# First edge stage of a two-layer graph network on one Trainium2 core: index columns and relative node columns held in SBUF and copied per chunk

## The chip, the cores and the metric

The kernel runs on one core of one Trainium2 chip. The metric is the device time of one execution in microseconds (us). The engines of the core are TensorE (PE), VectorE (DVE), ScalarE (ACT) and GpSimd (POOL); SyncE (SP) issues transfers. Transfers issued by SP and ACT and those issued by POOL run on the same 16 DMA engines.

## What is computed

The reference is two graph transformer layers over 6250 nodes of 256 features, with 206,250 edges sorted by destination. The part that this change touches is the first layer's edge attention:

```
src, dst = edges in order of dst                # 206250
s = einsum('edh,edh->eh', q[rows], k[cols])     # rows = dst, cols = src, 8 heads of 32
m = segment_max(s, rows);  e = exp(s - m[rows])
z = segment_sum(e, rows);  attn = e / z[rows]
out = segment_sum(attn[:, None, :] * v[cols], rows)
x = x + out @ Wo + bo + mix(xn)
```

After it come a routed feed-forward layer, a second layer with a mean over neighbours, linear attention and a second routed layer whose gates come from a graph attention over 139,264 edges. None of that is touched.

## The kernel before

The program is a row of stages. The ones that matter here lie between 860 and 4260 us of the span:

- `plan_steps` (L646 to L820) cuts the sorted edges into steps of 256 edges, each inside one window of 128 destination nodes, and makes the tables that the edge stage reads. On PE it transposes two of them (L741), so that a table with one step per partition becomes one with an edge of a tile per partition: the destination relative to the window (`rel`, written to `turned` negated, L817) and the source node (`lsf`, written to `turned_i` as integers, L819). Both are 128 partitions by 1792 columns of four bytes, one column per tile of 128 edges. SP writes them to DRAM as `SRCI` and `RELT` (L713, L714) and the stage ends when five such writes have landed (L715).
- `window_masks` (from L823) is a small stage that makes constants.
- `edge_attention` (L857 on) is the first edge stage. It runs over 107 chunks of 16 tiles of 128 edges (8 steps). `chunks` (L900) writes two chunks in front, a loop with two chunks in its body, and the last few at the end. All buffers of a chunk are double (index `s`).

What each engine does for a chunk, in the order of its own program:

- SP (`ahead`, `behind`, L929 to L942) reads with DMA: `oht`, the relative nodes of 2048 edges broadcast to all partitions (1 MB); `idx`, 16 columns of `SRCI` (L934); `relt`, 16 columns of `RELT` (L936); then `t3` and `flg` for the scans (L940, L941). Each waits until the chunk two before has released its buffer.
- POOL (`gather`, L960) fetches key and value rows of the source nodes: 16 indirect DMAs (L965), each with 128 rows of 2080 bytes, whose row numbers are one column of `idx`. It first waits for `idx` to land (L961). Each four gathers wait until PE has used up the four tiles two chunks earlier (`agg_ps`, L963). So a chunk has two stretches of eight gathers: groups 0 and 1, which are free once PE has done the first sums of the same-parity chunk before it, and groups 2 and 3, freed in the following body.
- ACT makes one-hot matrices with Abs and Relu: of `oht` (L977, L982) and of the nodes per tile (`far_edges`, L991, with a column of `relt` as bias; `mask_edges`, L998). It also takes the exponential (L1036, L1037) and copies the sums out of PSUM (`keep`, L1002).
- PE expands the queries of the window (L1067), transposes scores (L1074) and weights (L1113), spreads carries (L1101, L1106), makes the factor of a continued window (L1118, L1119), and sums messages (L1082, L1083, L1087); `agg_ps` counts the last of these.
- DVE multiplies and reduces scores (L1145, L1147), scans for the maxima (L1153 to L1177), weighs values (L1192) and rescales the open window (L1182, L1199).

The order on each engine is written out by hand. On ACT, in the body of chunk i, the first two of the 16 L991 of chunk i+1 stand between a `keep` and the exponential of chunk i; the wait for `relt` stands ahead of them. `at(eng, sem, c, per, i)` (L639) waits until chunk c has reached its count; inside the loop it is a wait against a register. `loaded` (L58) is the same for a DMA.

Of the kernel before, what the change touches and what calls it, by code (L numbers as in the profile page):

```python
# [57 lines left out]
def loaded(eng, sem, t, s, per=1, slots=2):  # L58


    wait_reg(eng, sem, (t - s) * (16 * per // slots) + 16 * per)
# [584 lines left out]
def plan_steps(nc, k, w):  # L646

    with ExitStack() as c:
# [17 lines left out]
        flg = sb("flg", [P, SC, 2, 4])  # L666
        turned = sb("turned", [P, NSP, 2])
        turned_i = sb("turned_i", [P, NSP, 2], I32)
        psA = c.enter_context(nc.psum_tensor("p_psA", [P, 512], F32))
# [17 lines left out]
        def _(sp):  # L687
# [24 lines left out]
            sp.wait_ge(turn_sb, 2)  # L712
            sp.dma_start(k.SRCI, turned_i[:].rearrange("p s g -> p (s g)")).then_inc(kept, 16)  # L713
            sp.dma_start(k.RELT, turned[:].rearrange("p s g -> p (s g)")).then_inc(kept, 16)  # L714
            sp.wait_ge(kept, 16 * 5)  # L715

# [140 lines left out]
def edge_attention(nc, k, w):  # L857
# [5 lines left out]
    with ExitStack() as c:  # L863
# [22 lines left out]
        set_done, table_in, q_in, zeroed = sem("set_done"), sem("table_in"), sem("q_in"), sem("zeroed")  # L886
        rel_in, t3_in, flg_in, idx_in, relt_in = ([sem(f"{n}_in{s}") for s in range(2)] for n in (
            "rel", "t3", "flg", "idx", "relt"))
        kv_in = [[sem(f"kv_in{s}_{g}") for g in range(4)] for s in range(2)]
# [5 lines left out]
            "exp_done", "oht_done", "oh_done", "oht_abs", "oh_abs", "fac_done"))  # L895
        x_step = sem("x_step")
        block = c.enter_context(nc.Block())
# [27 lines left out]
        @block.sync  # L925
        def _(sp):
            sp.dma_start(acc[:, 1:NT + 1, 0:C], k.Q.rearrange("(t p) c -> p t c", p=P)).then_inc(q_in, 16)

            def ahead(i, s):  # L929
                at(sp, q_ps, i - 2, 4, 3)  # L930
                sp.dma_start(oht[:, s, :], k.REL.rearrange("s e -> (s e)")[bass.ds(i * CT * P, CT * P)].partition_broadcast(P))\
                    .then_inc(rel_in[s], 16)
                at(sp, s_done, i - 2, 4, 3)
                sp.dma_start(idx[:, s, :], k.SRCI[:, bass.ds(i * CT, CT)]).then_inc(idx_in[s], 16)  # L934
                at(sp, oh_done, i - 2, 2, 1)
                sp.dma_start(relt[:, s, :], k.RELT[:, bass.ds(i * CT, CT)]).then_inc(relt_in[s], 16)  # L936

            def behind(i, s):
                at(sp, x3_done, i - 2, 1, 0)
                sp.dma_start(t3[:, s, :], k.T3D[bass.ds(i * CT, CT), :].unsqueeze(1).to_broadcast([CT, HEADS, TW])).then_inc(t3_in[s], 16)  # L940
                sp.dma_start(flg[:, s].rearrange("p t f -> p (t f)"),  # L941
                             k.FLG.rearrange("t f -> (t f)")[bass.ds(i * CT * 4, (CT + 1) * 4)].partition_broadcast(HEADS)).then_inc(flg_in[s], 16)  # L942
            ahead(0, 0)
            ahead(1, 1)
            behind(0, 0)

            def body(i, s):
                if inside(i + 2):
                    ahead(i + 2, s)
                if inside(i + 1):  # L950
                    behind(i + 1, 1 - s)
            chunks(sp, body)

        @block.gpsimd
        def _(pool):
            pool.memset(acc[:, NT + 1, :], 0.0).then_inc(zeroed, 1)
            pool.memset(acc[:, 0, :], 0.0).then_inc(zeroed, 1)
            pool.memset(acc[:, 1:NT + 1, C:VW], 0.0).then_inc(zeroed, 1)

            def gather(i, s):  # L960
                loaded(pool, idx_in[s], i, s)  # L961
                for g in range(4):
                    at(pool, agg_ps, i - 2, CS, 2 * g + 1)  # L963
                    for t in range(4 * g, 4 * g + 4):
                        pool.indirect_dma_start(kv[:, s, t, :], None, k.KV,  # L965
                                                bass.IndirectOffsetOnAxis(ap=idx[:, s, t:t + 1], axis=0)).then_inc(kv_in[s][g], 16)
            chunks(pool, gather)

        @block.scalar
        def _(act):  # L970
# [13 lines left out]
            def far_edges(i, s, tiles):  # L984
                if tiles[0] == 0:
                    loaded(act, relt_in[s], i, s)
                    at(act, agg_ps, i - 2, CS, CS // 2 - 1)
# [1737 lines left out]
def program(nc, w, out, scratch):  # L2725
    k = Core()
    with ExitStack() as c:
# [12 lines left out]
        k.REL, k.T3D = scratch("REL", [NSP, STEP]), scratch("T3D", [2 * NSP, TW])  # L2740
        k.FLG, k.SRCI, k.RELT = scratch("FLG", [2 * NSP, 4]), scratch("SRCI", [P, 2 * NSP], I32), scratch("RELT", [P, 2 * NSP])
        k.STEPB, k.STEPI, k.FIRST = scratch("STEPB", [NSP]), scratch("STEPI", [NSP], I32), scratch("FIRST", [NSP])
# [23 lines left out]
        with ExitStack() as cg:  # L2766
# [3 lines left out]
            with ExitStack() as ce:  # L2770
                k.QA = ce.enter_context(nc.sbuf_tensor("QA", [P, NT + 2, VW], F32))
                with ExitStack() as cw:
                    k.step_i, k.step_r = (cw.enter_context(nc.sbuf_tensor(n, [1, NSP], I32)) for n in ("step_i", "step_r"))
                    k.selh, k.maskj, k.selT, k.negpart = (cw.enter_context(nc.sbuf_tensor(n, s, F32)) for n, s in (
# [45 lines left out]
```

## Time and profile before

| | us |
|---|---|
| Median of 3 runs (13223.25 to 13242.68) | 13238.97 |
| The profiled execution, whole | 13243.9 |
| Its span, first to last instruction | 13242.3 |
| First edge stage, first SP issue to last L991 start | 951 to 4235 |
| Busy in the whole span: PE / DVE / ACT / POOL | 6677 / 6328 / 2226 / 6040 |

The page's busy shares are means over stages with different limits: none of the engines is over half busy in the whole span. The chain that ended last, in the page, is that of the final feed-forward stage and says nothing of the edge stage. What bounds the edge stage has to be read from the waits and the order of events in it. In rows of the trace, a bracket such as `[4.69 <-PE e_psA L1087]` gives the idle time ahead of the instruction and what ended it; `issue` stands for time in which nothing visible was waited for, `remote` for a semaphore that came long after the instruction that raises it seemed done.

### The profile page before, as it was taken

The page shows a single profiled execution, that of the slowest core. Times are in us where ns is not written, and L with a number is a line of the kernel's source. Part 1 is how long each engine was busy: PE and PEld are TensorE (multiplying, and loading weights), DVE is VectorE, ACT ScalarE, POOL GpSimd, SP SyncE. Part 2 cuts the span into 40 slices and gives each one's busy share as a digit, 9 for nine tenths or more (in the row PEclk, how much of TensorE's full clock was granted, in tenths as well). Part 3 has the DMA queues.
Part 4 walks back from the last instruction along what each step waited for, and adds up shares of the span by engine and source line. Part 5 has one row for each costly group of instructions (what it writes and reads, how often), then busy time and mean ns, then how long its engine had stood idle before and what let it go on. Part 6 is the DMA issues. An engine that isn't in the chain of part 4 may idle for free. (4 is left out here: it accounts for less than half of the span.)

```text
span 13242.3 us, 124947 instructions
## 1 busy us (share of the span) xinstructions
PE 6677.3 (50%) x26695; PEld 4426.6 (33%) x26696; DVE 6328.2 (48%) x12364; ACT 2226.2 (17%) x4818; POOL 6040.3 (46%) x6038
## 2 busy tenths in 40 slices
PE   4647777777777659989996000000024200000399
PEld 2325555555555535555554000000013100000277
DVE  5855565656665757777777233333332100005133
ACT  1114444444443101111110000000000000000122
POOL 1215444444443045444444666666631477772300
PEclk8768898998998878998997555555555555555699
DMA  1136555555554211111112455545531111111100
GB/s 66 50 105 184 180 183 176 183 181 180 182 183 148 74 56 36 32 38 32 32 36 67 148 177 170 177 168 170 175 123 50 47 9 9 9 9 43 26 16 16
DMA packets 583830, 1307.39 MB, mean 99 GB/s; under 512 B 206400, under 2 KB 354069, under 8 KB 553239
## 3 DMA queue, kind: packets, MB, share of 16 engines
q0 software_dynamic: 296736, 704.79, 19.2%
q1 hardware_dynamic: 250581, 321.56, 7.2%
q10 hardware_dynamic: 36288, 278.41, 5.7%
q8 instruction: 96, 1.57, 0.1%
q14 instruction: 129, 1.06, 0.0%
HBM read 1001.64 MB, written 309.87 MB: 99 GB/s over the span
## 5 line engine op out<-in xcount | busy, mean ns | idle before, releaser
L965 POOL DMA_INDIRECT e_kv<-KV,e_idx x1712 | 1619.0, 946 | 1656.5 <-PE e_psA L1087 1141.1
L2304 POOL DMA_INDIRECT s_x<-XN,s_idx x1612 | 1555.7, 965 | 928.9 <-issue 520.7
L1592 POOL DMA_INDIRECT SD<-o_pay,o_pos x1024 | 1156.3, 1129 | 1191.4 <-DVEq L45 733.8
L2018 PE MATMUL psY_f<-w_f,H_f 128*128 128x512 f32 x3200 | 1457.2, 614 | 31.2 <-issue 31.2
L2546 POOL DMA_INDIRECT t_gr<-G,t_idx x1088 | 1131.9, 1040 | 362.7 <-issue 362.7
L2325 DVE SCALAR_TENSOR_TENSOR s_x<-s_x,s_same 128x256 f32<-128x256 f32 x1488 | 723.6, 486 | 1136.1 <-issue 992.9
L1309 PE MATMUL j_ps_s<-j_diag_s,ones 128*128 128x128 f32 x2 | 0.8, 502 | 2466.0 <-DVE j_diag_s L1272 2466.0
L1067 PE MATMUL e_psQ<-QA,e_oht 128*128 x3424 | 891.1, 406 | 193.4 <-issue 124.3
L1309 PE MATMUL j_ps_g<-j_diag_g,ones 128*128 128x128 f32 x2 | 0.8, 500 | 1790.5 <-DVE j_diag_g L1272 1790.5
L2018 PEld LDWEIGHTS psY_f<-w_f,H_f 128*128 128x128 f32 x3200 | 621.6, 197 | 788.7 <-issue 788.7
L1087 PE MATMUL e_psA<-QA,ident 128*128 x1712 | 659.4, 472 | 357.6 <-DVE QA L1199 182.5
L1309 PEld LDWEIGHTS j_ps_s<-j_diag_s,ones 128*128 128x128 f32 x2 | 0.5, 311 | 2466.4 <-DVE j_diag_s L1272 2466.4
L1067 PEld LDWEIGHTS e_psQ<-QA,e_oht 128*128 128x128 f32 x3424 | 664.4, 202 | 385.0 <-issue 291.4
L1636 DVE SCALAR_TENSOR_TENSOR o_eq<-o_dbf,o_dc,o_ahead 128x128 bf16<-128x128 f32 (+7 forms) x1024 | 776.9, 817 | 12.5 <-ACT o_dbf L1677 1.4
L2569 DVE COPY t_g<-t_gr 128x384 f32 (+1 forms) x68 | 24.5, 360 | 1537.0 <-DMA t_gr<-G,t_idx 1537.0
L1082 PE MATMUL e_psA<-e_kv,hold 128*128 128x264 f32 x1712 | 623.2, 450 | 104.1 <-issue 73.1
L1926 DVE SCALAR_TENSOR_TENSOR xg_f<-psY_f,gate_f,xg_f 128x256 f32<-128x256 f32 x600 | 290.3, 484 | 671.5 <-PE psY_f L2013 503.9
L1192 DVE TENSOR_TENSOR e_kv<-e_psP,e_kv 128x1056 f32<-128x1056 f32 x428 | 534.7, 1250 | 141.3 <-remote 114.9
L1309 PEld LDWEIGHTS j_ps_g<-j_diag_g,ones 128*128 128x128 f32 x2 | 0.5, 313 | 1790.6 <-DVE j_diag_g L1272 1790.6
L1083 PE MATMUL e_psA<-e_kv,hold 128*128 128x264 f32 x1712 | 591.9, 431 | 0.0
L1002 ACT ACTIVATE QA<-e_psA 128x264 f32 x856 | 331.8, 388 | 1488.5 <-PE e_psA L1087 1246.8
L1145 DVE TENSOR_TENSOR e_kv<-e_psQ,e_kv 128x1024 f32<-128x1024 f32 x428 | 521.5, 1218 | 123.8 <-DVE e_xs L1177 47.5
(558 smaller groups left out, 12608.3 us busy)
## 6 DMA issues: line engine op xcount, KB each, us to landing
PS<-s_x ACTq DMA_DIRECT2D x124, 1664.0 KB
e_oht<-REL SPq DMA_DIRECT2D x107, 1024.0 KB
o_db<-in_L_ffn_edge_index_dram ACTq DMA_DIRECT2D x128, 512.0 KB
e_kv<-KV,e_idx POOLq DMA_INDIRECT x1712
s_x<-XN,s_idx POOLq DMA_INDIRECT x1612
hold<-T3D SPq DMA_DIRECT2D x107, 192.5 KB
t_gr<-G,t_idx POOLq DMA_INDIRECT x1088
SD<-o_pay,o_pos POOLq DMA_INDIRECT x1024
```

What stands on the lines that cost most here:

```text
L965: pool.indirect_dma_start(kv[:, s, t, :], None, k.KV, bass.IndirectOffsetOnAxis(ap=idx[:, s, t:t + 1], axis=0)).then_inc(kv_in[s][g], 16)
L1067: last = pe.matmul(psQ[:, g % 2, t % 4, :], oht[:, s, t * P:(t + 1) * P], acc[:, bass.ds(b[t // 2 % 4] + 1, 1), 0:C].rearrange("p a n -> p ...
L1082: pe.matmul(psA[:, u % 2, 0:VW], oh[:, s, 2 * u, :], kv[:, s, 2 * u, C:KW], start=True, stop=False)
L1083: pe.matmul(psA[:, u % 2, 0:VW], oh[:, s, 2 * u + 1, :], kv[:, s, 2 * u + 1, C:KW], start=False, stop=False)
L1087: pe.matmul(psA[:, u % 2, 0:VW], k.ident[:], acc[:, bass.ds(r[u % 4], 1), :].rearrange("p a n -> p (a n)"), start=False, stop=True).then_i ...
L1192: dve.tensor_tensor(v, p, v, ALU.mult).then_inc(pv_done, 1)
L1592: pool.indirect_dma_start(self.k.SD, bass.IndirectOffsetOnAxis(ap=self.pos[:, s, j:j + 1], axis=0), self.pay[:, s, j, :], None).then_inc(s ...
L1636: last = dve.scalar_tensor_tensor(out=self.scrap(j), in0=self.dbf[:, s, 0:n], scalar=self.dc[:, j:j + 1], in1=self.ahead[:, SB * P - n:], ...
L2018: last = pe.matmul(psY[:, h, b, :], H[:, m, i * P:(i + 1) * P], w2[:, m, e:e + 2, :].rearrange("p e n -> p (e n)"), start=(m == 0), stop=( ...
L2304: pool.indirect_dma_start(x[:, s, j, :], None, k.XN2, bass.IndirectOffsetOnAxis(ap=idx[:, s, j:j + 1], axis=0)).then_inc(x_in[s], 16)
L2325: ins = dve.scalar_tensor_tensor(out=x[:, s, j, :], in0=prev, scalar=same[:, j:j + 1], in1=x[:, s, j, :], op0=ALU.mult, op1=ALU.add)
L2546: pool.indirect_dma_start(gr[:, s, j, :], None, k.G, bass.IndirectOffsetOnAxis(ap=idx[:, s, j:j + 1], axis=0)).then_inc(g_in[s], 16)
```

## The change

The two turned tables are made in two SBUF tensors that live through the edge stage (`k.relt`, `k.src_i`), and are no longer written to DRAM. In the edge stage POOL copies the 16 index columns of a chunk from `k.src_i` into `idx` ahead of the first gather of the chunk, and ACT copies the 16 columns of `k.relt` into `relt` ahead of the first L991. SP's two reads per chunk are gone.

```diff
-        turned = sb("turned", [P, NSP, 2])
-        turned_i = sb("turned_i", [P, NSP, 2], I32)
+        turned, turned_i = (x[:].rearrange("p (s g) -> p s g", g=2) for x in (k.relt, k.src_i))
...
             sp.wait_ge(turn_sb, 2)
-            sp.dma_start(k.SRCI, turned_i[:].rearrange("p s g -> p (s g)")).then_inc(kept, 16)
-            sp.dma_start(k.RELT, turned[:].rearrange("p s g -> p (s g)")).then_inc(kept, 16)
-            sp.wait_ge(kept, 16 * 5)
+            sp.wait_ge(kept, 16 * 3)
...
-                at(sp, s_done, i - 2, 4, 3)
-                sp.dma_start(idx[:, s, :], k.SRCI[:, bass.ds(i * CT, CT)]).then_inc(idx_in[s], 16)
-                at(sp, oh_done, i - 2, 2, 1)
-                sp.dma_start(relt[:, s, :], k.RELT[:, bass.ds(i * CT, CT)]).then_inc(relt_in[s], 16)
...
             def gather(i, s):
-                loaded(pool, idx_in[s], i, s)
                 for g in range(4):
                     at(pool, agg_ps, i - 2, CS, 2 * g + 1)
+                    if g == 0:
+                        at(pool, s_done, i - 2, 4, 3)
+                        pool.tensor_copy(idx[:, s, :], k.src_i[:, bass.ds(i * CT, CT)]).then_inc(idx_done, 1)
+                        at(pool, idx_done, i, 1, 0)
...
                 if tiles[0] == 0:
-                    loaded(act, relt_in[s], i, s)
+                    at(act, oh_done, i - 2, 2, 1)
+                    act.activation(relt[:, s, :], k.relt[:, bass.ds(i * CT, CT)], ACT.Copy).then_inc(relt_done, 1)
+                    at(act, relt_done, i, 1, 0)
                     at(act, agg_ps, i - 2, CS, CS // 2 - 1)
```

POOL, the loop of the edge stage, first chunk of the body, before (the DMA rows are the gathers into `e_kv`; `ISA` and `REGISTER_ALU` compute the value that a wait is compared with):

```order
L904 UNCONDITIONAL_BRANCH
L904 ISA
L43 ISA
L965 DMA e_kv<-KV,e_idx 128x520 x4
L43 REGISTER_ALU
L965 DMA e_kv<-KV,e_idx 128x520 x4
L43 REGISTER_ALU
L965 DMA e_kv<-KV,e_idx 128x520 x4
```

And now:

```order
L901 UNCONDITIONAL_BRANCH
L901 ISA
L43 ISA
L958 ISA
L958 COPY e_idx<-src_i 128x16
L43 REGISTER_ALU
L961 DMA e_kv<-KV,e_idx 128x520 x4
L43 REGISTER_ALU
L961 DMA e_kv<-KV,e_idx 128x520 x4
L43 REGISTER_ALU
L961 DMA e_kv<-KV,e_idx 128x520 x4
```

The copy stands behind the wait for PE's sums and ahead of the first gather, with two further register operations of its own.

ACT, the first body, from the one-hot work on `e_oht` to the exponential `e_E`, before:

```order
L982 ACTIVATE e_oht<-e_oht,ones 128x1024
L991 ACTIVATE hold<-iota,e_relt 128x128 x2
L1036 ACTIVATE e_E<-e_R 128x128
L1037 ACTIVATE e_fx<-e_fd 8x1
L982 ACTIVATE e_oht<-e_oht,ones 128x1024
```

And now:

```order
L978 ACTIVATE e_oht<-e_oht,ones 128x1024
L983 ACTIVATE e_relt<-relt 128x16
L989 ACTIVATE hold<-iota,e_relt 128x128 x2
L1034 ACTIVATE e_E<-e_R 128x128
L1035 ACTIVATE e_fx<-e_fd 8x1
L978 ACTIVATE e_oht<-e_oht,ones 128x1024
```

The copy of `relt` stands ahead of the two L991 and so ahead of the exponential.

## Rows read from the trace of the kernel before

**Rows 1.** Busy time of each engine in the middle of the edge stage.

```profile
core 0: us, PE busy (x) PEld busy (x) DVE busy (x) ACT busy (x) POOL busy (x), PEclk, DMA share, GB/s
1100.00:4100.00 3000.00, 2366.91 (x8847) 1692.41 (x8846) 1806.55 (x2856) 1402.55 (x3144) 1486.75 (x1573) 0.91 0.59 181
```

**Rows 2.** Groups by line, 950 to 4230 us: busy, mean ns, idle before and releaser.

```profile
L965 POOL DMA_INDIRECT e_kv<-KV,e_idx x1712 | 1619.0, 946 | 1656.5 <-PE e_psA L1087 1141.1 <-issue 492.4 <-DMA e_idx<-SRCI 23.0
...
L1199 DVE TENSOR_TENSOR QA<-QA,e_psX 128x264 f32 x106 | 45.5, 429 | 348.3 <-remote 319.3 <-issue 26.0 <-PE e_psX L1119 3.0
...
L1161 DVE TENSOR_TENSOR_SCAN e_xs<-e_flg,e_xs,e_psX 8x16 f32<-8x16 f32 x106 | 24.9, 235 | 361.9 <-remote 343.3 <-PE e_psX L1101 11.7 <-issue 6.8
...
L1182 DVE SCALAR_TENSOR_TENSOR e_gm<-ident,e_fx 8x8 f32<-8x8 f32 x106 | 22.4, 211 | 61.6 <-ACT e_fx L1037 31.3 <-issue 30.2
```

**Rows 3.** One stretch of eight gathers in order of time, and what resumed behind it.

```profile
2494.78 0.94 POOL L965 DMA_INDIRECT e_kv<-KV,e_idx  x1 [7.19 <-PE e_psA L1087]
...
2501.80 0.71 SPq L936 DMA_DIRECT2D e_relt<-RELT  x1
...
2503.53 0.94 POOL L965 DMA_INDIRECT e_kv<-KV,e_idx  x1 [0.30 <-issue]
...
2505.49 0.69 SPq L940 DMA_DIRECT2D hold<-T3D  x1
...
2506.32 0.23 DVE L1161 TENSOR_TENSOR_SCAN e_xs<-e_flg,e_xs,e_psX 8x16 f32<-8x16 f32 x1 [4.50 <-remote]
...
2509.17 0.94 POOL L965 DMA_INDIRECT e_kv<-KV,e_idx  x1 [4.69 <-PE e_psA L1087]
```

**Rows 4.** POOL's stretches with a gap after the first gather: the first and the last.

```profile
1180.39 0.94 POOL L965 DMA_INDIRECT e_kv<-KV,e_idx  x1 [5.43 <-PE e_psA L1087]
1183.04 0.94 POOL L965 DMA_INDIRECT e_kv<-KV,e_idx  x1 [1.71 <-issue]
...
1195.51 0.94 POOL L965 DMA_INDIRECT e_kv<-KV,e_idx  x1 [4.03 <-PE e_psA L1087]
...
3868.38 0.95 POOL L965 DMA_INDIRECT e_kv<-KV,e_idx  x1 [3.79 <-PE e_psA L1087]
...
3883.48 0.96 POOL L965 DMA_INDIRECT e_kv<-KV,e_idx  x1 [4.01 <-PE e_psA L1087]
```

**Rows 5.** ACT around the exponential, and DVE behind it, in order of time.

```profile
2514.49 0.39 ACT L1002 ACTIVATE QA<-e_psA 128x264 f32 x1 [2.04 <-PE e_psA L1087]
2514.78 0.68 ACT L991 ACTIVATE hold<-iota,e_relt 128x128 f32<-128x128 f32 x2
...
2515.56 0.19 ACT L1037 ACTIVATE e_fx<-e_fd 8x1 f32<-8x1 f32 x1
...
2515.96 0.21 DVE L1182 SCALAR_TENSOR_TENSOR e_gm<-ident,e_fx 8x8 f32<-8x8 f32 x1 [1.49 <-ACT e_fx L1037]
```

**Rows 6.** Small operations of POOL in other stages, groups by line and form.

```profile
L447 POOL TENSOR_TENSOR cr<-cn,half 128x2 f32<-128x2 f32 x1 | 0.7, 698 | 4.4 <-DVE cn L510 4.4
...
L1849 POOL TENSOR_SCALAR im_f<-iota 128x8 f32<-128x8 f32 x1 | 0.2, 250 | 446.9 <-POOLq L128 446.9
...
L723 POOL MEMSET p_T<- 128x14 f32 x1 | 0.1, 112 | 0.0
```

**Rows 7.** The end of the plan and the first chunk, in order of time.

```profile
937.83 2.86 DVE L819 CAST p_turned_i<-p_psS 128x128 int32<-128x128 f32 x14 [3.40 <-PE p_psS L741]
...
947.44 0.24 POOL L836 IOTA wm_col_i<- 128x128 int32 x1 [32.64 <-ACTq L825]
...
974.53 2.19 ACT L977 ACTIVATE e_oht<-e_oht,negpart 128x1024 f32<-128x1024 f32 x2 [115.45 <-DMA e_oht<-REL]
974.94 0.96 POOL L965 DMA_INDIRECT e_kv<-KV,e_idx  x1 [23.05 <-DMA e_idx<-SRCI]
...
1011.49 1.22 DVE L1145 TENSOR_TENSOR e_kv<-e_psQ,e_kv 128x1024 f32<-128x1024 f32 x1 [15.05 <-remote]
...
1015.70 0.42 DVE L1153 TENSOR_TENSOR_SCAN e_FL<-hold,e_psX 128x128 f32<-128x128 f32 x1 [1.73 <-PE e_psX L1074]
```

More of the change, by code:

```diff
@@ L886, in edge_attention @@
         set_done, table_in, q_in, zeroed = sem("set_done"), sem("table_in"), sem("q_in"), sem("zeroed")
-        rel_in, t3_in, flg_in, idx_in, relt_in = ([sem(f"{n}_in{s}") for s in range(2)] for n in (
-            "rel", "t3", "flg", "idx", "relt"))
+        rel_in, t3_in, flg_in = ([sem(f"{n}_in{s}") for s in range(2)] for n in (
+            "rel", "t3", "flg"))
         kv_in = [[sem(f"kv_in{s}_{g}") for g in range(4)] for s in range(2)]
@@ L895, in edge_attention @@
             "exp_done", "oht_done", "oh_done", "oht_abs", "oh_abs", "fac_done"))
-        x_step = sem("x_step")
+        x_step, idx_done, relt_done = sem("x_step"), sem("idx_done"), sem("relt_done")
         block = c.enter_context(nc.Block())
@@ L2740, in program @@
         k.REL, k.T3D = scratch("REL", [NSP, STEP]), scratch("T3D", [2 * NSP, TW])
-        k.FLG, k.SRCI, k.RELT = scratch("FLG", [2 * NSP, 4]), scratch("SRCI", [P, 2 * NSP], I32), scratch("RELT", [P, 2 * NSP])
+        k.FLG = scratch("FLG", [2 * NSP, 4])
         k.STEPB, k.STEPI, k.FIRST = scratch("STEPB", [NSP]), scratch("STEPI", [NSP], I32), scratch("FIRST", [NSP])
@@ L2772, in program @@
                 with ExitStack() as cw:
+                    k.relt = cw.enter_context(nc.sbuf_tensor("relt", [P, 2 * NSP], F32))
+                    k.src_i = cw.enter_context(nc.sbuf_tensor("src_i", [P, 2 * NSP], I32))
                     k.step_i, k.step_r = (cw.enter_context(nc.sbuf_tensor(n, [1, NSP], I32)) for n in ("step_i", "step_r"))
```

## The prediction

> **What bounds the kernel now.** I read the page first and set it aside: its chain that ended last lies in the final stage, and its shares are means over unlike stages. Then the busy times of the edge stage alone [rows 1]. There TensorE is busy 2367 of 3000 us (79%), VectorE 60%, POOL 50%, ACT 47%, at a granted clock of 0.91, and the DMA engines are busy 59% of the time with 181 GB/s. Nothing is full, so the stage goes by a loop of waits. The groups by line say which [rows 2]. POOL's 1712 gathers stand 1656.5 us idle ahead of themselves, 1141.1 of it until PE's sums (L1087), 492.4 as the fixed 0.3 us between gathers, and only 23.0, once, for the index columns. DVE in turn idles 361.9 us ahead of L1161 and 348.3 ahead of L1199, nearly all "remote": PE's matmuls L1101 and L1119 are shown as done, but their semaphores come 3.2 and 3.0 us later in the mean (343.3 and 319.3 over 106 chunks). So POOL waits for PE, and DVE waits for a PE that answers late.
>
> The order of time shows how these hang together [rows 3]. Eight gathers start at 2494.78, the last at 2503.53 ends at 2504.47; DVE's L1161, idle for 4.50 us, starts at 2506.32, 1.85 us behind it; PE's next sums let POOL start again at 2509.17. From the start of one stretch to that of the next are 14.39 us, of which POOL works 9.7. If PE answers only once the gathers drain, the length of POOL's stretch is itself on the path.
>
> The trace holds an experiment on that. In nine chunks a gap of 1.7 us instead of 0.3 stands after the first gather of groups 0 and 1, so that the stretch ends 1.4 us later; the first and the last of them are in [rows 4]. The next stretch then starts 15.12 and 15.10 us after the first gather, against 14.39 in the undisturbed chunk. So 1.4 us more of POOL cost about 0.7 us of the chunk: a slope of at least 0.5. It isn't proven to be 1, and I use 0.7 below because other undisturbed chunks may be shorter than the one shown.
>
> **Part 1, POOL's copy.** One copy of 128x16 integers per chunk now stands between the wait for PE's sums and the first of the eight gathers of groups 0 and 1, 107 times. No row shows it. From below: a write of 128x14 takes 112 ns and an operation on 128x8 takes 250 ns [rows 6]; from above: 698 ns for a two-input one on 128x2, which is a power function and so costlier. I take 0.25 us. Around it come the wait for `s_done`, the copy's own completion, and two more register operations; the gather's own 0.3 us of issue isn't saved, since it depends on the copy. I take another 0.3 to 0.4 us, so 0.6 us together, with ends at 0.15 and 1.2. What is queued behind: the eight gathers, then groups 2 and 3, whose wait for PE (4.69 us in [rows 3]) would hide the copy altogether if PE didn't follow the gathers. With the slope of 0.7, 0.42 us per chunk, +45 us; with the ends, 0 (slope 0) to 1.2 x 1.0 x 107 = +128.
>
> The removed wait for `idx` gives nothing in the loop: its 23.0 us are all in the first chunk.
>
> **Part 2, ACT's copy.** It stands between the `keep` that ends at 2514.88 and the two L991 at 2514.78 (they overlap: ACT pipelines) [rows 5]. A tiny activation takes 0.19 us (L1037). L991 can't overlap the copy that it reads, so 0.19 plus the semaphore's way back, about 0.35 us, are put ahead of the exponential. In [rows 5] that is on the path: DVE's L1182 waited 1.49 us for L1037. Over the stage L1182 idled 61.6 us [rows 2]; at 1.49 each those are some 41 chunks of 106, and I count half of all, 50. So 0.35 x 50 = +17 us; from 0, if the late PE hides it all, to 0.5 x 107 = +53.
>
> **Part 3, SP.** Two issues with their waits go, per chunk. SP is not on the path: `t3` and `flg` are read a chunk ahead, and `oht` waits for PE. They will now be issued earlier, right behind `oht`. I count nothing, and keep the opposite view as a rival. The bytes are 16 KB of some 5.5 MB a chunk.
>
> **Part 4, the end of the plan and the first chunk.** The last turned table is ready at 940.69 and the next stage starts at 947.44 [rows 7]; between them SP waits for the last writes. Two of the five, 1.8 MB, go. I take 4 us off, between 0 and 6. In the edge stage POOL's first gather waited 23.05 us for index columns queued behind the read of the queries, 6.4 MB; it will start some 22 us earlier. But ACT and PE wait for that same queue (ACT's first operation at 974.53), and now up to 32 gathers of 266 KB share the DMA engines with it. What may come early is the part behind: DVE's fourth score at 1011.49 after 15.05 us, the first scan at 1015.70. I take 7 us off, between +10 and -25.
>
> **Sum.** +45 + 17 - 4 - 7 = +51 us on a profiled execution of 13243.9 us (span 13242.3), which lies 4.9 us above the median of 13238.97. I predict 13290 for the median, +0.39%. Differences under 0.2%, 26 us, are about what a measurement of this kernel can't tell from none.
>
> A rule speaks for a dearer copy. The Trainium skill (SBUF — State Buffer, "SBUF: two separate sides") says that VectorE and GpSimd share a port pair under an exclusive lock, held for a whole instruction, and that a GpSimd operation that reads SBUF is also shut out by a VectorE operation with two SBUF inputs. No GpSimd operation in the edge stage reads SBUF as a compute operand before the change, so no row bears on it. By that rule the copy could wait for one of the small two-input scans; the large DVE operations of this stage have one input in PSUM, so the sum would stay as it is. It would become the second rival only if the large ones shut it out too.
>
> The same section says that a DMA cannot be slowed by compute and that PE never waits for a port. The rows disagree at least in effect: L1161 and L1199 wait over 3 us for a PE whose matmuls seemed done, behind stretches of gathers [rows 2, 3]. The measurement decides; were it not so, Part 1 would be 0.
>
> **Rivals.**
>
> *Hidden (no change).* PE's late answers are its own matter, POOL's stretch merely keeps time with it, and the wait of 4 to 5 us ahead of groups 2 and 3 swallows the copy. For: that wait is there in [rows 3] and both of [rows 4]. Against: the stretch with the gap of 1.4 us more is still followed by a wait of 4.03 and 4.01 us against 4.69, so at least half of the gap was passed on and not swallowed. Time: 0 + 0 to 17 - 11, about 13240.
>
> *Lock or slow copy (slower).* The copy takes one DVE operation more. In POOL's wake-up DVE is in the midst of operations of 1.22 us (L1145 in [rows 7]). Half of one per chunk, 0.6 us at slope 0.7 to 1, is another 45 to 65 us: 13290 + 55 = 13345. From 0.7 us a copy on this would decide.
>
> *SP's small reads hold PE up (faster).* In [rows 3] SP issues `relt` at 2501.80 for 0.71 us, comes to its next issue only at 2505.49, and PE's semaphore reaches DVE at 2506.32, within a microsecond. If the 256 rows of 64 bytes for `idx` and `relt` cause the delay, removing them frees the 343.3 us ahead of L1161, of which PE's own slower clock and the scans take some. Half of it, -170, with -11 and +45: 13239 - 136, about 13105. It decides if the delay at L1161 falls under 2 us. Against: L1199 has the same delay (319.3 us in 106) at a place in the chunk where SP reads neither, since its two issues come behind the last scores of the chunk and the masks. So gathers alone suffice.
>
> *The change isn't what it says.* The order shows the copies in place and SP's reads gone, so I give this nothing.
>
> **Chances.** Forecast 0.50, with a range of its own from 13262 to 13330 (copy from 0.3 to 0.9 us, ACT's from 0 to 35). Hidden 0.22, lock or slow copy 0.10, SP's reads 0.18. Slower by over 0.2% (above 13265): nearly all of the forecast and the lock, 0.58 less a little for a dear first chunk's gain, 0.56. Faster by over 0.2%: the last rival and a share of hidden, 0.19. The rest 0.25. The range that leaves out no more than 2 in 10 takes in hidden, forecast and most of the lock, and the upper part of the faster rival, where a third of the delay goes instead of half: 13165 to 13370.
>
> **What would show it.** Period of a chunk, from POOL's first gather of one to that of the next, up by 0.5 to 0.6 us. A POOL copy of 0.2 to 0.3 us between 0.5 and 0.8 us ahead of the first gather; then eight gathers and L1161 still 1.7 to 1.9 us behind their end. The idle time ahead of L1161 and L1199 at 3.4 and 3.3 us a chunk as before; if L1161's alone is unchanged, that is against SP's reads. ACT's copy at 0.2 us and L1182's idle time up by 10 to 20 us in all. POOL's first gather some 25 us earlier, the first scan 5 to 15 us earlier. The prediction is wrong if L1161's delay shrinks, if POOL's idle time ahead of groups 2 and 3 shrinks by as much as the copy costs, or if the stages behind the edge stage move.

## The result, and the profile after

The changed kernel took 13275.67 us (median of 6 runs, 13248.76 to 13296.93) against 13231.47 us of the kernel before on the same chip (6 runs, 13217.87 to 13248.16). The ratio is 1.0033, 95% interval 1.0021 to 1.0044: slower by 44 us, where 51 us had been predicted. The profiled execution of the changed kernel is the fastest of its six (13248.76 us, span 13247.2), so its sum is nearer to the kernel before than the medians are; below it is read by stages, not by its end.

The middle of the edge stage, busy time by engine, answers to [rows 1]; one chunk fewer fits into it (97 first scans against 98), at the same granted clock:

```profile
1100.00:4100.00 3000.00, 2334.84 (x8746) 1668.14 (x8746) 1787.65 (x2815) 1408.30 (x3207) 1492.96 (x1652) 0.91 0.58 178
```

The groups by line answer to [rows 2] (L961 is the gather, L958 and L983 the two copies, L1159, L1166, L1180, L1197 the operations that were L1161, L1168, L1182, L1199):

```profile
L961 POOL DMA_INDIRECT e_kv<-KV,e_idx x1709 | 1621.0, 949 | 1009.9 <-issue 472.0 <-PE e_psA L1085 456.6 <-POOL e_idx L958 81.3
...
L1197 DVE TENSOR_TENSOR QA<-QA,e_psX 128x264 f32 x106 | 45.5, 429 | 382.4 <-remote 285.8 <-PE e_psX L1117 87.6 <-issue 8.9
L1159 DVE TENSOR_TENSOR_SCAN e_xs<-e_flg,e_xs,e_psX 8x16 f32<-8x16 f32 x106 | 24.9, 235 | 251.1 <-DMA MV<-q 186.3 <-issue 51.7 <-PE e_psX L1099 13.0
L1180 DVE SCALAR_TENSOR_TENSOR e_gm<-ident,e_fx 8x8 f32<-8x8 f32 x106 | 22.8, 215 | 76.5 <-ACT e_fx L1035 43.7 <-issue 32.8
L983 ACT ACTIVATE e_relt<-relt 128x16 f32 (+1 forms) x107 | 22.2, 207 | 0.0
L958 POOL COPY e_idx<-src_i 128x16 int32 (+1 forms) x106 | 20.5, 194 | 646.2 <-PE e_psA L1085 608.3 <-DVE e_S L1145 37.9
L1166 DVE TENSOR_TENSOR e_junk<-e_psX,maskj 128x32 f32<-128x32 f32 x106 | 19.9, 188 | 218.1 <-PE e_psX L1104 218.1
```

The same line as the last one, in the kernel before:

```profile
L1168 DVE TENSOR_TENSOR e_junk<-e_psX,maskj 128x32 f32<-128x32 f32 x106 | 19.8, 187 | 75.0 <-PE e_psX L1106 72.6 <-issue 1.4
```

The reader is to see three things. POOL's wait for PE has moved in part to the copy: 608.3 us ahead of it and 456.6 ahead of the later gathers, 1064.9 together, against 1141.1. DVE's wait ahead of the carries shrank from 361.9 to 251.1 us, and DVE's next wait for PE, a few operations on, grew from 75.0 to 218.1. And L1180 idles 76.5 us instead of 61.6, as foreseen. (The profile names a releaser `MV<-q` ahead of L1159; that transfer belongs to a stage whose last one is issued at 859.8 us, and the 186.3 us are a wait of the kind shown as `remote` before.)

The plan's end and the first chunk, in order of time, answer to [rows 7]; the last two rows, of the loop, show the price of the copy: 0.79 us from its end to the first gather, 0.98 us from its start. Not all of that is new, since a gather that waits for PE itself starts late as well. By the semaphore's own times in the traces, the first gather came 0.77 us behind PE's answer before and comes 1.36 us behind it now (mean of 93 chunks): 0.59 us later.

```profile
941.59 0.24 POOL L833 IOTA wm_col_i<- 128x128 int32 x1 [27.91 <-ACTq L822]
...
946.46 0.99 POOL L961 DMA_INDIRECT e_kv<-KV,e_idx  x1 [0.27 <-POOL e_idx L958]
...
986.69 2.19 ACT L973 ACTIVATE e_oht<-e_oht,negpart 128x1024 f32<-128x1024 f32 x2 [128.93 <-DMA e_oht<-REL]
...
1004.00 0.42 DVE L1151 TENSOR_TENSOR_SCAN e_FL<-hold,e_psX 128x128 f32<-128x128 f32 x1 [0.64 <-PE e_psX L1072]
...
1018.41 0.19 POOL L958 COPY e_idx<-src_i 128x16 int32 x1 [31.99 <-PE e_psA L1085]
1019.39 0.98 POOL L961 DMA_INDIRECT e_kv<-KV,e_idx  x1 [0.79 <-POOL e_idx L958]
```

The plan ends 5.9 us earlier (947.44 to 941.59), POOL's first gather comes 28.5 us earlier, ACT's first operation 12.2 us later, and the first scan 11.7 us earlier. From the first scan to the last, 3220.9 us have become 3253.3: +32.4. At the end of the edge stage the changed kernel is 20.7 us behind; this one execution then wins 15.8 back in stages whose instructions are the same, and the medians, 44 us apart, say that it is not typical.

Where in the chunk the time is lost is seen best in the mean place of each operation behind the chunk's first scan (L1153; mean over the 95 chunks from the 6th on, worked out from the starts in both traces), in us:

```
                                        before   after
first gather behind the scan (POOL)      0.37    0.85   +0.48
carries, first scan (DVE L1161)          5.92    4.83   -1.09
first store of sums (ACT L1002)          6.65    6.98   +0.33
operation behind M2 (DVE L1168)          8.61    8.95   +0.34
fourth store (ACT L1002)                12.77   13.08   +0.31
exponential (ACT L1036)                 13.64   14.35   +0.71
rescale of the window (DVE L1199)       20.67   21.09   +0.42
next chunk's first scan                 30.54   30.90   +0.36
```

The scan falls into a stretch of eight gathers, so the first row is the fifth gather of its stretch. Measured from the scan, POOL's gathers start 0.48 us later, and 0.34 of it is there when PE answers behind them: a slope of 0.7. Measured from PE's answer they start 0.59 us later, which makes the slope 0.6. ACT's copy then puts another 0.40 us between the fourth store and the exponential (0.87 to 1.27), and all but 0.02 of that is gone when the chunk closes, since the rescale waits for a late PE anyway. That is a reading of places, on one chip. The experiments were to show the parts one by one.

### The profile page after: what moved, and what is told of

Same layout as the page of the kernel before. It is cut to its first block and busy times, and to the rows that moved or that the text cites. A ratio compares the mean times of both kernels' runs of the same rounds, so it can differ in the third digit from the quotient of the medians.

```text
span 13247.2 us, 124895 instructions
## 1 busy us (share of the span) xinstructions
PE 6648.4 (50%) x26695; PEld 4413.0 (33%) x26696; DVE 6330.7 (48%) x12364; ACT 2250.5 (17%) x4925; POOL 6050.8 (46%) x6145
## 5 line engine op out<-in xcount | busy, mean ns | idle before, releaser
L961 POOL DMA_INDIRECT e_kv<-KV,e_idx x1712 | 1623.9, 949 | 1010.8 <-issue 472.6
L1993 PE MATMUL psH_f<-xT_f,w_f 128*128 128x320 f32 x1920 | 568.6, 458 | 21.4 <-ACT xT_f L1954 13.8
```

Of the source, the lines that this page charges most:

```text
L961: pool.indirect_dma_start(kv[:, s, t, :], None, k.KV, bass.IndirectOffsetOnAxis(ap=idx[:, s, t:t + 1], axis=0)).then_inc(kv_in[s][g], 16)
L1993: last = pe.matmul(psH[:, h, 0:HALF], w1[:, a, m * P:(m + 1) * P], xT[:, a, h * HALF:(h + 1) * HALF], start=(a == 0), stop=(a == KC - 1))
```

## The experiments

They ran on three other chips, and there the kernel before took 12173 to 12185 us, 1046 to 1059 us less than in the first comparison, with the same instructions. So the kernel before was profiled again. Its groups in the middle of the edge stage:

```profile
L965 POOL DMA_INDIRECT e_kv<-KV,e_idx x1547 | 1461.9, 945 | 1038.9 <-PE e_psA L1087 601.7 <-issue 437.2
...
L1161 DVE TENSOR_TENSOR_SCAN e_xs<-e_flg,e_xs,e_psX 8x16 f32<-8x16 f32 x96 | 22.6, 236 | 107.5 <-PE e_psX L1101 107.5
...
L977 ACT ACTIVATE e_oht<-e_oht,negpart 128x1024 f32<-128x1024 f32 x193 | 211.2, 1141 | 327.2 <-DMA e_oht<-REL 327.2
```

No wait is "remote" any more: DVE idles 1.1 us a chunk ahead of L1161, not 3.4. A chunk lasts 25.85 us, not 30.54. Every ratio below is against the kernel before on the same chip. All times of chunks and places are worked out as above, from the starts in the traces; the kernel before was profiled on one of the three chips only, so a place or period of another chip is compared with that one.

**The kernel before and the changed one again.** No edit.

> The kernel before, unchanged, for its profile on the chip on which the other runs were made: there its time is 12185 us against 13231 on the chip of the first comparison. Theory: the 1046 us are PE's late semaphores (remote waits of L1161 and L1199, 662 us in the edge stage) and what follows from them; the profile here shows no remote waits and a chunk of 25 to 26 us in place of 30.5.

> The changed kernel on the same chip as the runs before. If PE's late answers are what passes POOL's copy on, and they are absent here, the cost of the copy falls away: first scan 10 us earlier, loop within 20 us of before, the kernel 5 to 25 us below before. If the two copies add up from the single runs (-70 for POOL's alone, +62 for ACT's alone), it lies at -8 +-15 us.

Before: 12179.22 us (one run, the profiled one; the median of 21 others on that chip is 12174.52). Changed: 12186.92 us, ratio 1.0007 (0.9998 to 1.0016), chunk 25.80 us. On these chips the change costs nothing that can be told, where it cost 0.33% on the first.

**POOL's copy alone.** `relt` is read by SP as before.

```diff
+                sp.dma_start(relt[:, s, :], k.RELT[:, bass.ds(i * CT, CT)]).then_inc(relt_in[s], 16)
...
-                    act.activation(relt[:, s, :], k.relt[:, bass.ds(i * CT, CT)], ACT.Copy).then_inc(relt_done, 1)
+                    loaded(act, relt_in[s], i, s)
```

> Only the index columns stay in SBUF and are copied by POOL; the relative node columns are written to DRAM and read by SP as before. Theory (POOL's copy on the path, ACT's at nothing, SP's reads at nothing): the period of a chunk is up by about 0.3 us as with the whole change (30.52 to 30.85 us), the first scan 8 to 12 us earlier, the kernel 20 to 45 us above before. Rival A (ACT's copy is what costs): the loop as before, the kernel 5 to 12 us below before. Rival B (SP's small reads hold PE up): one of two is left, so L1161's delay would fall by half of what it fell with both.

12115.58 us against 12185.43, ratio 0.9946 (0.9933 to 0.9960), chunk 25.12 us. The copy that was to cost 45 us gains 70 here. The sign of Part 1 does not hold on this chip.

**ACT's copy alone.** `idx` is read by SP and awaited by POOL as before.

> Only the relative node columns stay in SBUF and are copied by ACT; the index columns go by DRAM and SP as before. Theory: the period of a chunk is that of before (30.5 us, within 0.1), the kernel from 5 us below to 10 us above before. Rival A (ACT's copy costs): period up by 0.15 to 0.3 us, the kernel 15 to 35 us above before.

12247.49 us, ratio 1.0052 (1.0038 to 1.0065), chunk 26.32 us. It costs 62 us, +0.47 a chunk: more than the copy in place (0.40), and so in every chunk and not in half of them. The change is thus a gain and a loss that nearly cancel: -70 + 62.

**SP's reads kept.** The changed kernel, with SP still writing both tables and reading both each chunk into tiles that nobody uses.

> The changed kernel, but the plan still writes both tables and SP still reads both per chunk, into tiles that nothing uses. Theory (SP's reads cost nothing in the loop): the period as in the changed kernel (30.85 us), the plan's end some 5 us later, the kernel 0 to 10 us above the changed one. Rival B (the removed reads gave something back, which hides part of the copies' cost): the period over 31.0 us and the kernel over 20 us above the changed one.

12193.0 us, ratio 1.0008 (0.9999 to 1.0017), against 1.0007 for the change without them. On these chips the reads are worth nothing that can be told, either way.

**POOL's copy three times.** In a chain, each waiting for the one before.

```diff
-                        pool.tensor_copy(...).then_inc(idx_done, 1)
-                        at(pool, idx_done, i, 1, 0)
+                        for n in range(3):
+                            pool.tensor_copy(...).then_inc(idx_done, 1)
+                            at(pool, idx_done, i, 3, n)
```

> The changed kernel with POOL's copy made three times in a row, each waited for. Theory (a later start of the gathers is passed on at 0.6 to 0.7): each extra copy with its wait takes about 0.4 us, so the period is up by another 0.45 to 0.6 us and the kernel by 45 to 65 us over the changed one. Rival C (POOL's copy is swallowed by the wait ahead of groups 2 and 3, and the loss comes from elsewhere): no change against the changed kernel. A slope of 1 would give 85 us.

12187.62 us, ratio 1.0004 (0.9995 to 1.0013), as with one copy. Later gathers are neither passed on here nor do they gain more: ACT's mask, which waits for the 1 MB read, starts 0.41 us behind the scan instead of 2.21, and the first store stays where it was, at 5.46. Once the read is out of the way, a still earlier one is worth nothing.

**Both copies moved.** POOL's copy for chunk i+1 stands behind the gathers of group 1 of chunk i, ACT's for chunk i+2 at the end of the body; and POOL's alone moved so.

```diff
+                    if g == 1 and inside(i + 1):
+                        fetch(i + 1, 1 - s)
...
                 if more:
                     mask_edges(i + 1, 1 - s, 1)
+                if most:
+                    fetch_relt(i + 2, s)
```

> The changed kernel with POOL's copy for the next chunk behind the gathers of group 1 (ahead of the wait for groups 2 and 3) and ACT's copy for the chunk after the next at the end of the body. Theory: both leave the path, only the earlier first chunk and plan stay, and ACT's part (+62 alone) goes: 30 to 80 us below the changed kernel on this chip. Rival: the order of gathers and not the copies matters, no change.

> Only POOL's copy is moved as in the run before; ACT's copy stays ahead of the exponential. Theory: if POOL's copy costs 0.3 us per chunk, 30 us below the changed kernel; if on this chip its delay of the gathers is what gains (POOL's copy alone gave -70), moving it loses that: 30 to 70 us above the changed kernel.

Both moved: 12190.21 us, ratio 1.0013 (1.0004 to 1.0022). Only POOL's moved: 12239.39 us, ratio 1.0050 (1.0037 to 1.0064). Where POOL's copy does not delay the gathers, its gain is gone and ACT's cost stands bare (65 us, as the 62 above); where neither delays anything, the kernel is the kernel before, within 16 us. The gain of 30 to 80 us over the changed kernel that was expected of moving both did not come, because POOL's copy on the way is worth as much as ACT's costs.

**ACT's copy moved, POOL's kept on the way.** This is the version to which these results point.

> The changed kernel with one thing moved: ScalarE's copy of the relative node columns stands at the end of the body of chunk i, for chunk i+2, and no longer ahead of the two exponentials; GpSimd's copy of the index columns stays on the way to the gathers. If the two copies' effects add up as the single ones did (GpSimd's copy alone -70 us, ScalarE's alone +62 us, ScalarE's moved off the way 0 to +15), this is 50 to 70 us faster than before (ratio 0.994 to 0.996). Rival, the gain of the copy on GpSimd hangs on the time at which ScalarE starts its masks: no change against before, ratio 1.000 to 1.001. On a chip where TensorE's semaphores come late behind the gathers, as on the first comparison's, the theory of the prediction (a later gather is passed on at 0.7) gives +20 to +50 us instead.

12111.07 us against 12173.95, ratio 0.9951 (0.9938 to 0.9965), 63 us faster than before. On this chip it beats both kernels; on the first it was not run.

**A pause.** Nothing of the change: `idx` is read by DMA, and POOL copies it once more, to a tile that nobody reads, before it gathers.

```diff
+                    if g == 0:
+                        at(pool, s_done, i - 2, 4, 3)
+                        pool.tensor_copy(idx_p[:, s, :], idx[:, s, :]).then_inc(idx_done, 1)
+                        at(pool, idx_done, i, 1, 0)
```

> The kernel before, index columns read by SyncE's DMA as before; GpSimd alone is given a copy of the same 128x16 columns from that tile to a tile that nobody reads, at the place where the change has its copy, and waits for it ahead of the first gather of each chunk. If what gains is the later start of the first gathers (by some 0.5 us), this is as fast as the kernel with GpSimd's copy alone: 50 to 75 us faster than before, ratio 0.994 to 0.996. If what gains is that the index columns come from a copy and not from a DMA, this loses or stays: ratio 1.000 to 1.004.

12109.23 us, ratio 0.9951 (0.9937 to 0.9965), chunk 25.14 us. So the later start of the gathers is enough for the gain, made by a copy that does no work. The groups of this kernel, same stretch and columns as those of the kernel before above (L969 is the gather, L981 was L977):

```profile
L969 POOL DMA_INDIRECT e_kv<-KV,e_idx x1593 | 1509.0, 947 | 813.1 <-issue 419.8 <-PE e_psA L1091 315.7 <-POOL e_idx_p L966 77.6
...
L981 ACT ACTIVATE e_oht<-e_oht,negpart 128x1024 f32<-128x1024 f32 x200 | 218.8, 1140 | 167.0 <-DMA e_oht<-REL 167.0
```

ACT's wait for the 1 MB read of `oht` fell from 327.2 us in 96 chunks (3.4 each) to 167.0 in 100 (1.7). Why, is in the order of time. One chunk of the kernel before on such a chip:

```profile
2486.82 0.94 POOL L965 DMA_INDIRECT e_kv<-KV,e_idx  x1 [2.17 <-PE e_psA L1087]
2488.07 0.94 POOL L965 DMA_INDIRECT e_kv<-KV,e_idx  x1 [0.30 <-issue]
2488.38 0.34 SPq L931 DMA_DIRECT2D e_oht<-REL  x1
...
2492.75 0.42 DVE L1153 TENSOR_TENSOR_SCAN e_FL<-hold,e_psX 128x128 f32<-128x128 f32 x1 [0.66 <-PE e_psX L1074]
...
2495.95 2.19 ACT L977 ACTIVATE e_oht<-e_oht,negpart 128x1024 f32<-128x1024 f32 x2 [3.18 <-DMA e_oht<-REL]
...
2498.84 0.39 ACT L1002 ACTIVATE QA<-e_psA 128x264 f32 x1 [0.70 <-PE e_psA L1087]
```

And one with the pause:

```profile
2498.22 0.19 POOL L966 COPY e_idx_p<-e_idx 128x16 int32<-128x16 int32 x1 [1.77 <-PE e_psA L1091]
2499.20 0.98 POOL L969 DMA_INDIRECT e_kv<-KV,e_idx  x1 [0.79 <-POOL e_idx_p L966]
2500.18 0.35 SPq L931 DMA_DIRECT2D e_oht<-REL  x1
...
2504.55 0.42 DVE L1157 TENSOR_TENSOR_SCAN e_FL<-hold,e_psX 128x128 f32<-128x128 f32 x1 [0.66 <-PE e_psX L1078]
...
2506.41 2.19 ACT L981 ACTIVATE e_oht<-e_oht,negpart 128x1024 f32<-128x1024 f32 x2 [1.83 <-DMA e_oht<-REL]
```

Two gathers of the stretch have been issued ahead of SP's read in the one (so in 88 of 97 chunks between 1100 and 3600 us), one in the other (98 of 99). From its issue until ACT starts are 7.57 us in the one and 6.23 in the other (mean over the stage 7.8 and 6.1). The difference, 1.3 us here and 1.7 in the mean, is of the size that the 266 KB of one gather take at the stage's 213 GB/s (1.25 us, an estimate). That one gather less ahead of it is the reason fits these numbers; it is an argument, and no run changes the order alone.

**ACT's copy three times.**

> The kernel before with ScalarE's copy of the relative node columns ahead of the exponentials, made three times in a chain; the index columns are read by DMA as before. With one copy it was 62 us slower than before. If ScalarE's time ahead of the exponentials is on the path that closes each chunk, each further copy with its wait (0.27 us or more) adds as much again: +120 to +190 us, ratio 1.010 to 1.016. If the first copy only moves the chunk into another pattern of the clock and the gathers, two more add little: ratio 1.004 to 1.007.

12316.89 us, ratio 1.0120 (1.0105 to 1.0136), chunk 27.02 us. Two more copies add 0.70 us a chunk, 0.35 each, where one starts 0.30 us behind the one before: the copy with its wait is passed on whole, and a little more. In this trace the copies are

```profile
L984 ACT ACTIVATE e_relt<-relt 128x16 f32 x279 | 59.4, 213 | 17.0
```

**The masks behind the stores.** The kernel before, with ACT's order alone changed, so that the late read no longer stands ahead of the first store.

```diff
-                if most:
-                    far_nodes(i + 2, s, 0)
-                    far_nodes(i + 2, s, 1)
                 for h in range(2):
                     if old:
                         keep(i - 1, 4 + h, before[h])
+                    if most:
+                        far_nodes(i + 2, s, h)
```

> The kernel before (both tables read by DMA, no copies), with ScalarE's order alone changed: in the body of a chunk the two halves of the absolute difference on the node row (they wait for SyncE's 1 MB read of REL for the chunk after next) no longer stand ahead of the first two stores of the aggregate into the accumulator but one behind each. Theory, from the mean places in the chunk in the traces of this kernel: on the chips with the 25.8 us chunk the read lands 3.4 us after the scan, 1.7 us later than with GpSimd's pause, and holds up ScalarE's stores, for which TensorE's next sums wait, by 0.7 us a chunk; with the stores ahead of it the wait is out of the way, and the kernel gains as much without any pause: 50 to 90 us faster than before, ratio 0.993 to 0.996, chunk period 25.0 to 25.3 us, the first store of a chunk 0.5 to 1 us nearer the scan. Rival, the pause gains by what it does to the gathers themselves or to TensorE's clock: ratio 0.999 to 1.003 here, period 25.8 or more. A mishap that would hide the theory: the masks, now later, hold up the third store (ratio up to 1.005).

12194.49 us, ratio 1.0018 (1.0009 to 1.0027), chunk 25.95 us: the gain did not come. The row and the places say how far the theory holds.

```profile
L977 ACT ACTIVATE e_oht<-e_oht,negpart 128x1024 f32<-128x1024 f32 x194 | 221.0, 1139 | 0.0
```

The wait for the read is gone (0.0 from 327.2), and the first store comes 0.37 us earlier, so the read did hold up that store. But the two masks, 2.3 us of ACT, now stand between the stores and the third one, which comes 0.12 us later than before, and the chunk ends 0.10 later. It is the mishap named in the expectation. The first half of the theory is borne out, the gain is not; how the two go together shows below.

Mean places behind the chunk's first scan on these chips, in us (the columns of a single copy are of one chip, the masks moved of another, the rest of the third; the mask's place is the landing of the read only where ACT waits for it, so not in the last column):

```
                          before  change  POOL's  pause   ACT's   3 ACT   masks
                                          alone           alone   copies  moved
first gather behind it     0.34    0.97    0.97    0.89    0.34    0.34    0.34
ACT's mask (read landed)   3.42    2.21    1.91    1.71    3.53    3.32    5.81
PE's M1 (L1101)            3.18    3.17    2.90    2.89    3.27    3.58    3.27
first store                5.90    5.46    5.18    5.20    5.96    6.06    5.53
fourth store              10.81   10.36   10.08   10.10   10.88   10.96   10.91
exponential               11.68   11.64   10.95   10.97   12.15   12.85   11.78
next chunk's first scan   25.85   25.80   25.12   25.14   26.32   27.02   25.95
```

Read the change as a sum: -0.44 at the first store, from the read that lands earlier; +0.41 from the fourth store to the exponential (0.87 to 1.28), from ACT's copy; -0.04 when the chunk closes. With POOL's copy alone there is a further -0.28, already at M1, a matmul behind the query expansions; the granted clock of the stage is then 0.98 of the full 2.4 GHz instead of 0.96:

```profile
1100.00:3600.00 2500.00, 2211.80 (x8961) 1564.66 (x8959) 1819.24 (x2889) 1422.88 (x3186) 1527.83 (x1692) 0.98 0.72 220
```

for the kernel with the pause, and for the kernel before

```profile
1100.00:3600.00 2500.00, 2182.19 (x8712) 1540.00 (x8711) 1769.55 (x2804) 1376.01 (x3098) 1461.88 (x1547) 0.96 0.70 213
```

The traces tell what that clock is worth. In some chunks it falls to 1.2 GHz once, between the first scan and M1, in the others it stays at 2.4 GHz there (PE's work ahead of it is alike in both: a third busy around the scan). The same places, for the two kinds of chunk apart (95 chunks each; in the kernel before the clock falls later in one more):

```
                              before   pause   change   masks moved
clock falls: chunks             52       35      53        57
  period                       26.08    26.03   26.44     26.53
  first store                   6.14     6.09    6.09      6.10
clock stays: chunks             42       60      42        38
  period                       25.50    24.61   25.00     25.09
  first store                   5.58     4.67    4.67      4.66
```

So the earlier read gains in the chunks whose clock stays, 0.9 us at the first store, by the pause, by the change and by the moved masks alike; where the clock falls, PE is late anyway (M1 at 3.4 to 3.7 us behind the scan and not at 2.6) and the read gains next to nothing. The gain of the pause, 0.71 us a chunk, has two parts: with as many falls as before it would be some 0.45 (an estimate from these rows), and the rest is that the clock falls in 35 chunks and not in 52. ACT's copy adds 0.4 in either kind of chunk and brings the falls back to 53, which is why the change as a whole gains nothing.

## Why the prediction was right, and where not

The time was right: +44 us measured, +51 predicted, with the sign, and 13275.67 us lies inside the likeliest case's own range. Its mechanism holds for the chip on which it was measured, as far as the places in one trace show it; how near the sum came is in part luck. Of its terms:

- **Part 1, POOL's copy, +45.** On the first chip: delay 0.59 us behind PE's answer where 0.6 was taken, of which 0.34 are passed on, a slope of 0.6 where 0.7 was taken, so 0.34 x 107 = +36. The 0.7 itself is partly luck. It came from setting two of the nine natural gaps [rows 4] against one undisturbed chunk of 14.39 us; the mean of the 78 chunks without any gap is 14.05 and of the nine 15.25, so that 1.4 us more of POOL cost 1.2, a slope of 0.85, and the copy was passed on less than the gaps. What was wrong is to take the slope as a property of the kernel: on the other chips PE's answers are not late, and the same delay gains 0.7 us a chunk alone, 0.5 beside ACT's copy (26.32 to 25.80). The rival with the other sign that I had was SP's reads; the transfer that did gain from less company, the read of `oht`, I had written off in Part 3 with "`oht` waits for PE".

  The gaps would have told it. From one chunk's first gather to the next, the nine chunks with the gap last 31.57 us against 30.39 on the first chip, and 25.66 against 25.85 on the later one, with the same program (the small gain there is not clear of chance; that there is no loss of 1.2 us is). On the first chip the read of `oht` came earlier too (ACT's mask at 2.47 us behind the scan and not at 3.07), but the first store, behind a PE that answers late, came 0.33 later.
- **Part 2, ACT's copy, +17.** The size was right (0.35 taken; 0.40 in place, 0.35 for each further copy), how often it is passed on was not. Half of the chunks were counted; by the places it is next to none on the first chip (+0.02 at the chunk's end) and all of them on the others (+62 us). The idle time ahead of L1182 told only who waits there, not whether the wait is given back later.
- **Part 3, SP, 0.** Shown on a later chip, by the kernel that keeps the reads; not on the first.
- **Part 4, -11.** The first scan came 11.7 us earlier, on the first chip. On the others it came later, 1000.05 to 1004.82: there ACT's first mask came 15.2 us later (972.2 to 987.4), while POOL's first gather came 25 us earlier (972.56 to 947.33). That those gathers hold back the read, since they share the DMA engines with it, is the prediction's own argument; no run parts the two.
- **The sum.** 36 + 2 - 12 = +26 by the traces, against +32.4 - 11.7 = +20.7 read at the end of the edge stage, and 44 (28 to 58 by the interval) by the medians. Some 20 us are not accounted for: they lie within what executions of one kernel differ by (48 us between the changed kernel's six), and stay open. That the sum hit 44 to within 7 is thus in part chance.

Of the rivals, *hidden* is right for the later chips in its result but not in its reason. *Lock or slow copy* is out: POOL's copy takes 193 to 201 ns in all 107 chunks, and starts at most 0.67 us behind PE's answer, where a gather took 0.77. By the rule on the shared port that the prediction quoted from the Trainium skill (SBUF — State Buffer, "SBUF: two separate sides") a copy could at times have had to wait for a DVE scan; no row here shows it. Nor do the late answers contradict what the prediction quoted from the same section of the Trainium skill, that a DMA cannot be slowed by compute and that PE never waits for a port: the rows show semaphores that come late, not a wait at a port. *SP's small reads hold PE up* stays undecided on the first chip. The prediction said it would be wrong if L1161's delay shrank. It did, by 1.1 us a chunk, and the time did not follow: DVE's next wait for PE, at L1168, grew by as much and a little more (75.0 to 218.1 us). The wait moved on by a few operations. The reads, kept, cost nothing on the later chips, but those have no such delay; whether the reads move it on the first one was not tried.

What stays open: the split between the two copies on the first chip rests on places in one trace, since no single-part kernel ran there; why semaphores come late on that chip; and why the clock falls in fewer chunks with the pause, and in as many as before once ACT's copy is there too.

## What to carry to other kernels

When an engine that issues transfers starts a little later, its transfers line up differently with those of others. A later start is not always a loss: here ACT's wait for a large read fell from 3.4 to 1.7 us a chunk with it, and that was worth more than the delay cost. Before a sum of small terms is trusted, ask of each whether the wait it feeds is given back before the loop closes, and do each part of the change alone: here -70 and +62 us hid behind a result of "no change". And a slope read from one chip's trace holds for that chip, and should be read from all the chunks that show it, against the mean of those that don't. Where a period is a mean of two kinds of chunk, as here by the clock, look at each kind before explaining the mean.

## What the runs showed of the hardware

- One program differs by 1046 us (8%) from chip to chip. Nearly all of it lies in three stages with gathers: 508, 390 and 121 us of the 1065 by which two profiled spans differ. In the last of these the gathers themselves take longer (L2546, 1040 ns in the mean against 944); in the second edge stage they take as long and stand idle longer. First the kernel before on the first chip, then on another:

```profile
L2304 POOL DMA_INDIRECT s_x<-XN,s_idx x1612 | 1555.7, 965 | 928.9 <-issue 520.7 <-DMA s_idx<-srci 408.2
L2325 DVE SCALAR_TENSOR_TENSOR s_x<-s_x,s_same 128x256 f32<-128x256 f32 x1488 | 723.6, 486 | 1136.1 <-issue 992.9 <-DVE s_x L2325 51.0
```

```profile
L2304 POOL DMA_INDIRECT s_x<-XN,s_idx x1612 | 1558.1, 967 | 535.8 <-issue 490.9 <-DMA s_idx<-srci 44.9
L2325 DVE SCALAR_TENSOR_TENSOR s_x<-s_x,s_same 128x256 f32<-128x256 f32 x1488 | 725.0, 487 | 159.2 <-DVE s_x L2325 7.0
```

- On the first chip PE's semaphores reach DVE over 3 us after the matmul seems done, behind stretches of gathers [rows 2, 3]; in the edge stage on the others no wait is `remote`. It is not a matter of PE alone: in the second edge stage each L2325 of the rows above waits, by the kernel's text, for nothing but a semaphore that DVE itself raises with the L2325 before. Ahead of these DVE idles 1136.1 us on the first chip, 2.3 us at a time in stretches while gathers are being issued, and 159.2 on the other; the profile puts most of it down to `issue`. That PE's lateness was "its own matter", as the rival *hidden* had it, is thus unlikely on the first chip.
- A POOL copy of 128x16 integers takes 194 ns, an ACT copy of the same size 207 ns. From POOL's copy to an indirect DMA that needs it are 0.79 us in the loop, where both waits are against register values, and 0.27 us in the first chunk.
- On the later chips a chunk in which the granted clock falls to 1.2 GHz ahead of M1 is 1.4 us longer than one in which it stays at 2.4 GHz, once the read is out of the way (26.03 against 24.61), and 0.6 us longer where it is not (26.08 against 25.50).
